# Second edge stage of a graph network: tanh in place of silu, a softmax chain over two steps, and selection matrices made by ScalarE

## The reference

```
ms = src_s[edge_src] + dst_s[edge_dst]
mv = src_v[edge_src] + dst_v[edge_dst]
w = h @ rw3 + roff                        # h: a small network on the edge scalars
...                                       # ds, dv: products of w, ms, mv and the edge's direction
ls, lv = _eq_lin(ds, dv, lin_ws, lin_bs, lin_wv)
alpha = ls[:, :H * A].reshape(e, H, A)
a = jnp.einsum('ehk,hk->eh', _smooth_leaky(alpha), alpha_dot)
amax = jax.lax.stop_gradient(jax.ops.segment_max(a, edge_dst, num_segments=n))
a = jnp.exp(a - amax[edge_dst])
a = a / (jax.ops.segment_sum(a, edge_dst, num_segments=n)[edge_dst] + 1e-12)
ns = jax.ops.segment_sum(vs * a[..., None], edge_dst, num_segments=n).reshape(n, H * H0)
```

## Time and profile before

| | |
|---|---|
| runs | 10468.27, 10474.15, 10480.74 us |
| the profiled execution's own time | 10483.94 us |
| its span | 10482.1 us |
| busy share of the span | PE 84%, DVE 75%, POOL 64%, ACT 49% |
| first edge stage, node updates | up to about 5659 us |
| second edge stage (the one changed) | about 5659 to 9800 us |
| last node update | from about 9810 us |

### The profile page before, as it was taken

One profiled execution on the slowest core, in us unless ns is written; L12 is line 12 of the kernel. 1 busy time (PEld: TensorE's weight loads), 2 busy tenths in 40 slices (PEclk: granted clock), 3 DMA queues, 4 the chain that ended last, 5 costly groups with the idle time before them and its releaser, 6 DMA issues. The chain is left out here.

```text
span 10482.1 us, 192677 instructions
## 1 busy us (share of the span) xinstructions
PE 8818.0 (84%) x34728; PEld 5222.1 (50%) x34728; DVE 7895.4 (75%) x15400; ACT 5096.8 (49%) x9268; POOL 6671.5 (64%) x4771
## 2 busy tenths in 40 slices
PE   0888888888888799999996888888888888888588
PEld 0444444444444222322233666676666667676333
DVE  3277777777777588888896888888888888888465
ACT  0176666666666311111112555555555555555355
POOL 4478888888888788888884445444544544444232
PEclk5599999999999899999997999999999999999699
DMA  5588888888888899999993444444444444444222
GB/s 199 180 162 168 167 165 166 166 167 166 168 165 167 171 224 227 230 224 230 225 235 97 124 130 127 124 129 124 126 124 130 126 126 128 125 126 125 67 76 58
DMA packets 1081323, 1616.13 MB, mean 154 GB/s; under 512 B 218498, under 2 KB 831885, under 8 KB 1025357
## 3 DMA queue, kind: packets, MB, share of 16 engines
q1 hardware_dynamic: 755862, 1273.87, 44.1%
q0 software_dynamic: 325056, 338.58, 20.5%
HBM read 1533.80 MB, written 444.07 MB: 189 GB/s over the span
## 5 line engine op out<-in xcount | busy, mean ns | idle before, releaser
L442 POOL DMA_INDIRECT sums<-e_total,e_place x1568 | 2494.2, 1591 | 592.7 <-DMA sums<-e_total,e_place 330.8
L1933 POOL DMA_INDIRECT e_rows<-TS,e_at x1568 | 1540.0, 982 | 2086.2 <-DVE e_m L1961 1334.2
L579 PE MATMUL ps<-e_win,e_pick 128*128 128x448 f32 x3136 | 1335.7, 572 | 168.3 <-DVE e_u L476 127.8
L579 PEld LDWEIGHTS ps<-e_win,e_pick 128*128 128x128 f32 x3136 | 614.1, 201 | 917.3 <-issue 834.0
L2124 PE MATMUL ps<-e_win,e_pick 128*128 128x160 f32 x3136 | 620.7, 324 | 349.3 <-DVE e_pick L1951 281.9
L2261 ACT ACTIVATE e_dT<-ps 128x512 f32<-128x512 f32 x1176 | 660.1, 598 | 372.2 <-PE ps L2135 352.0
L1094 POOL TENSOR_TENSOR n_zv<-n_zv,n_ast 128x1536 f32<-128x1536 f32 x200 | 751.4, 3757 | 134.5 <-DMA n_zv<-in_x_groups 122.7
L2124 PEld LDWEIGHTS ps<-e_win,e_pick 128*128 128x128 f32 x3136 | 487.9, 202 | 564.0 <-issue 403.3
L1299 PE MATMUL ps<-n_z,w_uss 128*64 128x512 f32 x1600 | 746.7, 610 | 22.9 <-DVE n_z L1142 21.9
L2261 ACT ACTIVATE e_oT<-ps 128x512 f32<-128x512 f32 x784 | 468.2, 597 | 603.0 <-PE ps L2163 488.7
L2135 PE MATMUL ps<-ident,e_d 128*128 128x128 f32 x4704 | 648.3, 274 | 125.4 <-ACT e_dT L2261 125.0
(11 more groups left out here) (439 smaller groups left out, 20048.0 us busy)
## 6 DMA issues: line engine op xcount, KB each, us to landing
e_win<-T SPq DMA_DIRECT2D x1568, 168.0 KB
n_z<-in_x_groups SPq DMA_DIRECT2D x400, 512.0 KB
n_zv<-in_x_groups SPq DMA_DIRECT2D x800, 192.0 KB
TOT<-e_tot SPq DMA_DIRECT2D x392, 352.0 KB, 2.6
e_row<-in_src_rows SPq DMA_DIRECT2D x98, 1024.0 KB
e_local<-LR SPq DMA_DIRECT2D x196, 512.0 KB
e_row<-in_dst_rows SPq DMA_DIRECT2D x98, 1024.0 KB
e_win<-TD SPq DMA_DIRECT2D x1568, 60.0 KB
```

What stands on the lines that cost most here:

```text
L442: pool.indirect_dma_start(sums[c], bass.IndirectOffsetOnAxis(ap=place[:, r % 4, c:c + 1], axis=0), total[:, r % 4, c, 0:MSG0], None, compu ...
L579: pe.matmul(g[:, c, :], pick[:, p, R * c:R * c + R], win[:, s, c, :], start=True, stop=True).then_inc(spread, 1)
L1933: pool.indirect_dma_start(rows[:, p, 0, c, :], None, TS, bass.IndirectOffsetOnAxis(ap=at[:, gp, col:col + 1], axis=0)).then_inc(rows_here[ ...
```

## The change

1. **Leaky unit.** ACT computes tanh(x/2) instead of silu(x), DVE combines as (tanh + 1.5) x instead of 0.25 x + silu, and the weight `ad` is scaled with 0.4 instead of 0.8. Same instructions, same sizes, same places.
2. **The group's chain over two steps.** DVE's `scans` move from r%4 = 0 to r%4 = 1, there between `sums` and `results`; `shift` moves to r%4 = 1, after `weigh`. PE's `tops_down` moves to r%4 = 1, after the third transpose. ACT's `weigh_up` stays at r%4 = 1 but moves from ahead of `results` to behind the second `keep_totals`. SP loads the next target numbers one step later.
3. **Selections.** DVE's comparison goes; ACT makes each selection in two instructions, |local - partition number| into `e1_apart_by` and then max(0, 1 - that) into `e1_pick`. They stand between the second `keep_totals` (or `weigh_up`) and keep 4. The second waits for the first, and the first for the selection before. `picked` is counted by ACT now, and PE's wait for it is the same.
4. A table for exp, tanh and others is loaded once ahead of the stage, and DVE writes the negated partition numbers once.

```
-            step(dve.tensor_scalar(W["ad"][:], W["ad"][:], 0.8, None, ALU.mult))
+            step(dve.tensor_scalar(W["ad"][:], W["ad"][:], 0.4, None, ALU.mult))
...
-                        if r % 4 == 1 and not i.before(4) and not (final and r == 5):
+                        if r % 4 == 2 and not i.before(4) and not (final and r == 6):
                             gate(sp, k)
                             sp.wait_ge(scanned, i.groups(0))
                             load_dh(1 - r // 4, t + r // 4)
...
-                    dve.scalar_tensor_tensor(out=silu[:, p], in0=alpha4, scalar=0.25, in1=silu[:, p], op0=ALU.mult, op1=ALU.add
+                    dve.scalar_tensor_tensor(out=silu[:, p], in0=silu[:, p], scalar=1.5, in1=alpha4, op0=ALU.add, op1=ALU.mult
...
                         if more:
                             sums(after)
+                        if r % 4 == 1 and not i.before(5):
+                            scans(i)
                         if not i.before(1):
                             results(i.plus(-1))
                         if more:
                             weigh(after)
-                        if r % 4 == 0 and not i.before(4):
-                            scans(i)
+                        if r % 4 == 1 and not i.before(5):
                             shift(i)
                         if not i.before(5):
                             members(i)
-                        if i.plus(3).within():
-                            selections(i.plus(3))
...
                         turn(i, 2)
+                        if r % 4 == 1 and not i.before(5):
+                            tops_down(i)
                         map_scalars(i)
...
-                        if r % 4 == 0 and not i.before(4):
-                            tops_down(i)
...
+                def selections(i):
+
+                    p, s, gp = i.r % 2, i.r % 4, i.r // 4
+                    gate(act, k)
+                    act.wait_ge(local_here[gp], i.uses(16, 16))
+                    if not i.before(1):
+                        gate(act, k)
+                        act.wait_ge(picked, i.n(1))
+                    act.activation(apart_by[:], local[:, gp, GT * R * s:GT * R * s + GT * R], ACT.Abs, bias=minus[:]
+                                   ).then_inc(differed, 1)
+                    if not i.before(2):
+                        gate(act, k)
+                        act.wait_ge(spread, i.n(2, 2, 2))
+                    gate(act, k)
+                    act.wait_ge(differed, i.n(1, 1))
+                    act.activation(pick[:, p, :], apart_by[:], ACT.Relu, scale=-1.0, bias=k["ones"][:, 0:1]).then_inc(picked, 1)
...
-                    act.activation(silu[:, p], alpha4, ACT.Silu).then_inc(outs, 1)
+                    act.activation(silu[:, p], alpha4, ACT.Tanh, scale=0.5).then_inc(outs, 1)
...
-                        if r % 4 == 1 and not i.before(5):
-                            weigh_up(i)
                         if not i.before(1):
                             results(i.plus(-1))
                         keep(i, 0)
...
                         if not i.before(6):
                             keep_totals(i, 1)
+                        if r % 4 == 1 and not i.before(5):
+                            weigh_up(i)
+                        if i.plus(3).within():
+                            selections(i.plus(3))
                         keep(i, 4)
```

More of the change, by code:

```diff
@@ L1748, in layer1_edges @@
         local, base = sb("e1_local", [128, 2, 16 * R], BF16), sb("e1_base", [1, 2, 4, 2 * GT], I32)
+        minus, apart_by = sb("e1_minus", [128, 1]), sb("e1_apart_by", [128, GT * R])
+        negated, differed = sem("e1_negated"), sem("e1_differed")
         win, pick = sb("e1_win", [128, 4, GT, X]), sb("e1_pick", [128, 2, GT * R])
@@ L1942, in _ @@
             def _(dve):
[L1943 to L1952, removed]
                 def sums(i):
@@ L2082, in _ @@
                 dve.memset(win[:], 0.0).then_inc(blank, 1)
+                dve.tensor_scalar(minus[:], iota[:, 0:1], -1.0, None, ALU.mult).then_inc(negated, 1)
                 dve.memset(hh[S:128], 0.0).then_inc(ones_set, 1)
@@ L2086, in _ @@
                 dve.wait_ge(ones_set, 2)
-                for r in range(3):
-                    selections(At(0, r))
                 sums(At(0, 0))
@@ L2304, in body @@
                             keep_totals(i, 1)
+                        if r % 4 == 1 and not i.before(5):
+                            weigh_up(i)
+                        if i.plus(3).within():
+                            selections(i.plus(3))
                         keep(i, 4)
+                act.preload_act_table_set("exp_and_others")
+                act.wait_ge(negated, 1)
+                selections(At(0, 0))
+                selections(At(0, 1))
                 for r in range(2):
@@ L2309, in _ @@
                         keep_far(At(0, r), half, far2(At(0, 0), half))
+                selections(At(0, 2))
                 passes(act, body)
```

## The result

Seven runs of the changed kernel took 10358.24 to 10425.99 us, median **10382.28**; the kernel before, run beside it, 10474.15. The ratio is 0.9909, 95% interval 0.9886 to 0.9931. It is faster, by 92 us; 349 were forecast (10125), and 10382 lies above the range.

What follows compares the result with a forecast made beforehand. No engine was full; waits between engines set 41.70 us a group. The chain gave 38.1: 3.6 x 96 = 347 us, plus 2.6 for two table loads, about 349 off 10483.9, so 10125 as median; range 10010 to 10260.

Steps and rivals of the forecast that it cites:

- The chain itself: Waits between engines in a group of four steps, summed by starts of DVE's `results`: 38.1 us for 41.7; chance 0.69.
- usual steps: PE's steps 2 to 3 and 3 to 0, with PE waiting for ACT's selection: 9.17 us each, formerly 8.51.
- step 1 to 2: DVE's results and shift, then ACT's exponential, copy and selection, then PE: 9.95 us, PE held some 1.8.
- PE's `tops_down`: With the scans a step later, it was to find its input ready.
- A: Rival: PE finds ACT's selection ready, usual steps stay 8.51 us; 36.1 us a group, 9930 us; chance 0.09.
- C: Rival: ACT becomes the bound, by table loads or slow instructions; one load a step gives 10560 us; chance 0.04.
- Rival B: PE's clock falls after idle time, 1.6 us each: 10200 us with half the groups, 10280 with all; chance 0.16.
- POOL multiplies after the exponential: POOL's product comes late in ACT's step, but PE reads it more than 2 us later: no new wait.
- Tanh's term: ACT's two table loads a group go, 2.6 us inside DVE's 3.3 us wait; only two loads counted separately, -2.6 us.
- The rule against this part: Selections on ACT: relu belongs on VectorE; moving them loses 1.7 us a group, some 160 us.
- The side calculation: Comparison left on DVE, 0.40 us a step, all signals in time: 36.4 us a group, near 9970 us.
- DVE waiting only at `by_y`: Sign of being right: DVE waits there 0.9 to 1.4 us and nowhere in the scans.

Runs made afterwards that it cites:

- shifted kernel: The changed kernel with 70 more empty instructions ahead of ACT's loop and 50 ahead of DVE's, nothing else altered: 10294.45 us, 0.9796 of the kernel before.

## Why the prediction was wrong

- **The chain itself held** where nothing else happened. Groups with neither DVE's gap nor a fall take 37.96 us (38.09 in the shifted kernel) against 38.1, usual steps 9.03 against 9.17, ACT's instructions 0.71 and 0.72 against 0.72, no table load is in the loop, and tanh took 0.38. The idle time in step 1 to 2 is the forecast 1.8 us only without the multiplication (1.8 to 2.0 in 94 of 96 groups). PE's `tops_down` did not always find its input ready: it waited up to 1.5 us, 34 times from 6200 to 9400. A and C are out.
- **The first step that failed** is the one that left PE's clock out of the sum. Rival B had a chance of 0.16, against it stood that "PE was busy right up to it", and every step was taken at full clock. The clock fell in 56 of 96 groups (50 in the second run of the changed kernel). The price of a fall was right, 1.6 us against 1.72 measured without the multiplication; its number was B's "half of the groups" and more. That is 1.1 us a group at most, some 100 us. (The 41.70 us of before contain 0.9 at most of the same kind; the sum dropped these by taking its slots from steps at full clock.) This is read from the granted clock and from groups with and without a fall; no run changed the clock alone.
- **The second** is "POOL multiplies after the exponential [...] PE reads the product more than 2 us after that: no new wait". It asked only whether PE gets the product late. POOL does wait now, and its multiplication falls upon other DVE instructions than before. All of DVE's slots (3.68, 3.96) were taken as constants from rows that hold only for the old meeting of the two engines. Leaving the multiplication out is worth 1.07 us a group; half of that is already in the falls above, so 0.5 us a group comes on top.
- **A term that the sum did not have** is the program's layout. I counted the instructions that run, not where they lie. It is worth 0.8 to 1.0 us a group, 90 to 120 us, as measured by moving the loops.
- Together: 38.1 and 1.1, 0.5 and 0.9 are 40.6, where 40.47 was measured.
- With the layout and the multiplication taken away the group is 38.43, 0.33 above the forecast. 0.9714 of 10474.15 is 10175: 50 us above 10125, and inside the range. 24 groups with a fall are left, at 39.72 us; the other 72 take 38.00.
- **Tanh's term** I did not put in the sum by itself, rightly: 1.67 us a group came of 2.56.
- **The rule against this part was right.** The side calculation (36.4 us with the comparison on DVE) missed by the collision alone (37.49). That the clock would not fall in that version was luck: nothing in the reckoning said so. The range's lower half had no reason; its upper end should have left room for what the profile of before can't show.
- "DVE waiting only at `by_y`" was wrong by the 52.6 us of issue gaps.

## What to carry to other kernels

Sort the steps or groups of a profile by the granted clock before comparing kernels: a mean of 0.97 for 0.98 hid that more than half of the groups had a fall of some 1.7 us, and two versions differed by 2.0 us a group of which only 0.6 was their work. When a change moves one engine's wait, ask what that engine does next and beside whom: a POOL instruction that slides by two microseconds can double the length of DVE instructions it never met before. Then ask whether the longer instruction is on the path, for it can also cost nothing. And compare the instruction packets of the two profiles first: if they more than double without more work, the loops have moved across a boundary, and a few empty instructions ahead of them tell how much that costs. An instruction given to an engine with spare time still costs its full length if it stands just ahead of what another engine waits for; here half of it moved into a wait of the same engine, together with an earlier shift, turned a loss into a gain.

## What the hardware showed that I had not expected

- DVE's 0.41 us instruction took up to 2.2 us beside POOL's multiplication, and POOL's 1.26 took 1.85 the other way round. The held DVE instruction ends a fixed time after POOL's (0.29 us for L2018), also where its recorded start is the earlier one. In groups without a fall of the clock 2.6 us of this cost 0.1.
- A fall of PE's clock costs 1.7 us where PE is on the path (39.72 against 38.00 us without the multiplication). Falls stood in 0, 1, 24, 41, 50, 54, 56 and 84 of 96 groups in the eight profiles of the chips like the first.
- A loop on DVE that needs refetching costs a gap of 1.36 us (up to 1.7) in every pass, with some 4.7 instruction packets more a pass for each engine concerned.
- The same program took 6 to 7 per cent longer on three of five chips, and the changes were worth other amounts there: tanh 0.3 to 0.6 per cent instead of 1.5, the whole change 3.0 to 3.1 instead of 0.9 to 1.2.
